# Token attention in a four-layer gated block: mask on four diagonal pieces, division after the weighted sum, head-wise exponentials, and the routing of two chunks inside the second attention

## What is computed

```python
x = x + tanh(g_xattn[1]) * L1_xattn(layernorm(x), ctx, ...)   # "attention(1)"
x = x + tanh(g_ffn[1])   * L1_ffn(layernorm(x), ...)          # experts, top 2 of 8
x = x + tanh(g_xattn[2]) * L2_xattn(layernorm(x), ctx)        # token attention
x = x + tanh(g_ffn[2])   * L2_ffn(layernorm(x), ...)          # "ffn2"

def L2_xattn(q, k, v):       # per token: its 16 heads attend to one another
    scores = einsum('bsqd,bskd->bsqk', qh, kh) / sqrt(8)       # 16 x 16 per token
    scores = where(tril(ones((16, 16))), scores, -1e18)
    return einsum('bsqk,bskd->bsqd', softmax(scores), vh)
```

## Time and profile before

| | |
|---|---|
| median of 3 runs | 1651.29 us (1651.13 to 1655.38) |
| the profiled execution | 1648.97 us, its span 1647.2 us |
| PE busy | 1186.6 us, 72% of the span |
| DVE busy | 1185.9 us, 72% |
| POOL busy | 790.9 us, 48% |
| ACT busy | 699.4 us, 42% |

### The profile page before, as it was taken

One profiled execution on the slowest core, in us unless ns is written; L12 is line 12 of the kernel. 1 busy time (PEld: TensorE's weight loads), 2 busy tenths in 40 slices (PEclk: granted clock), 3 DMA queues, 4 the chain that ended last, 5 costly groups with the idle time before them and its releaser, 6 DMA issues. The chain is left out here.

```text
span 1647.2 us, 31338 instructions
## 1 busy us (share of the span) xinstructions
PE 1186.6 (72%) x9741; PEld 789.5 (48%) x9741; DVE 1185.9 (72%) x3134; ACT 699.4 (42%) x1333; POOL 790.9 (48%) x834
## 2 busy tenths in 40 slices
PE   3788885459989869988886342404899886887886
PEld 1455554136656547756654111101566664544554
DVE  5677876686757635368888787885767565998997
ACT  1455554126656434455555111101566553333332
POOL 0223320003343137677777867873234323776876
PEclk9999998569999889989999665556999998999998
DMA  8455553253545023312112000310444420000000
GB/s 195 60 87 69 72 111 118 33 156 56 81 55 69 17 77 99 95 39 58 46 46 64 24 3 13 50 53 0 66 72 71 58 40 1 1 14 1 13 14 13
DMA packets 95266, 90.99 MB, mean 55 GB/s; under 512 B 8928, under 2 KB 85344, under 8 KB 94816
## 3 DMA queue, kind: packets, MB, share of 16 engines
q1 hardware_dynamic: 91040, 80.98, 26.2%
q0 software_dynamic: 4096, 8.40, 1.7%
HBM read 32.72 MB, written 18.87 MB: 31 GB/s over the span
## 5 line engine op out<-in xcount | busy, mean ns | idle before, releaser
L1533 DVE TENSOR_REDUCE neg_max<-bank 128x4 f32<-128x512 f32 x384 | 252.5, 686 | 129.2 <-PE bank L1053 127.1
L824 ACT ACTIVATE probs<-bank 128x512 f32<-128x512 f32 x384 | 212.5, 596 | 167.3 <-PE bank L1080 166.3
L1051 PE MATMUL bank<-mask_b,ident_b 128*128 128x512 bf16 x384 | 153.4, 400 | 67.0 <-DMA k_rows<-area 37.0
L555 POOL TENSOR_SCALAR rstd_a<-meanvar 128x4 f32<-128x4 f32 x48 | 12.0, 250 | 299.6 <-DVE meanvar L1489 221.0
L1053 PE MATMUL bank<-k_rows,q_rows 96*128 96x256 bf16 x768 | 153.9, 283 | 0.0
L817 ACT ACTIVATE q_rows<-bank 32x512 bf16<-32x512 bf16 x192 | 103.0, 582 | 107.3 <-PE bank L1063 103.9
L606 POOL CAST area<-area 128x1024 bf16<-128x1024 f32 x36 | 37.3, 1036 | 219.8 <-DMA k_rows<-area 167.1
L1070 PE MATMUL bank<-ident_b,mask_b 128*128 128x512 bf16 x384 | 134.3, 391 | 3.0 <-ACT probs L824 1.8
L1080 PE MATMUL bank<-q_rows,k_rows 128*128 128x128 bf16 x1536 | 135.4, 222 | 0.0
L1080 PEld LDWEIGHTS bank<-q_rows,k_rows 128*128 128x128 bf16 x1536 | 112.1, 99 | 27.7 <-issue 2.8
L1094 PE MATMUL bank<-probs,v_aug 128*32 128x128 f32 x3072 | 112.2, 287 | 0.8
(11 more groups left out here) (253 smaller groups left out, 3013.4 us busy)
## 6 DMA issues: line engine op xcount, KB each, us to landing
q_rows<-area SPq DMA_DIRECT2D x144, 128.0 KB
k_rows<-area SPq DMA_DIRECT2D x288, 64.0 KB
ctxT<-ctx_t SPq DMA_DIRECT2D x24, 256.0 KB, 6.7
moe_rows<-m2b SPq DMA_DIRECT2D x4, 1536.0 KB, 13.5
q_rows<-moe_rows SPq DMA_DIRECT2D x24, 256.0 KB, 3.2
moe_rows<-work SPq DMA_DIRECT2D x24, 256.0 KB, 2.4
room<-w_exp SPq DMA_DIRECT2D x1, 4352.0 KB, 13.6
mask_i<-mask SPq DMA_DIRECT2D x8, 256.0 KB, 8.5
```

Source lines behind the costliest of these rows:

```text
L824: act.activation(probs[j].rearrange("p a b -> p (a b)"), T_BANK[j % 2][:], ACT.Exp).then_inc(exp_done, 1)
L1051: pe.matmul(dst[:], ident_b[:], bcast(mask(b, t), 4), start=True, stop=False)
L1533: dve.tensor_reduce(neg_max[:, 4 * j:4 * j + 4], S_BANK[j % 2][:].rearrange("p (h k) -> p h k", h=4), AX.X, ALU.max, negate=True).then_inc ...
```

## The change

**Routing.** Chunk 0 is now routed wholly in the group `left` = 1 of `attention(1)` and chunk 1 in the group `left` = 0, up to its choice; chunk 1's ranks open PE's expert stage and its `put` opens DVE's. The scatter of chunk 0 stands on POOL at the head of the group `left` = 0, ahead of the bias additions. In the blocks only chunks 2 and 3 are left: statistics in blocks 0 and 1, turns and logits in blocks 1 and 3, choice and places in blocks 2 and 4. Chunk 1's scatter is split in two, with the inverse deviation of chunk 3 between the halves. Chunk 3's rows move to the room of the token products, so `products(0)` waits for its scatter. `FIRST_STEP` is 8: tiles 0 to 15 run in blocks, 16 to 31 in the tail, and the first four groups of ffn2 come one tile later in the tables.

**Token attention.** The mask is added to the 4 × 4 pieces on the diagonal only (64 scores; the rest of `tok_raw` is filled with the masked value once). `probabilities` is gone. The weighted product takes the exponentials themselves, in two buffers that alternate, and waits for `token_exp`; in `combine` DVE makes the sum and the reciprocal ahead of its wait for the weighted product, and a new product of 128 × 128 with the reciprocal stands behind the reductions. For n ≥ 16 there is no subtraction: ACT makes 16 exponentials, one per head, with the negated maximum as bias. The factor 1/√8 moves into the norm ahead of the products.

**POOL's order.** A half of the next group's gather stands between products(n+1) and weighted(n), not behind weighted(n).

```diff
-FIRST_STEP = 9
+FIRST_STEP = 8
+TAIL = NK - FIRST_STEP
+        tok_weights = (tok_e, tok_p)
...
 # POOL, attention(1)
+                        if a == 1 and left == 0:
+                            scatter(0)
                         if not is_first:
                             for t in range(TG):
                                 add_bias(TG * (gr - 1) + t)
-                        if a == 1 and left == 0:
+                        if a == 1 and left == 1:
                             route_std(1)
-                            scatter(0)
...
 # POOL, weighted(n)
-                pool.wait_ge(tok_probs, n + 1)
+                pool.wait_ge(tok_exp, n + 1)
...
 # POOL, feed_forward1_and_tokens
-                scatter(1)
+                scatter(1, range(TG))
                 route_std(3)
+                scatter(1, range(TG, TC))
...
+                    if g + 1 < NG and t < 2:
+                        gather(g + 1, range(2 * t, 2 * t + 2))
                     for events in (FFN2_STATS, NEXT_STATS):
                         if n in events:
                             at += 1
                             inv_std(at)
                     weighted(n)
-                    if g + 1 < NG:
-                        if t < 2:
-                            gather(g + 1, range(2 * t, 2 * t + 2))
...
 # ACT, token_exp(n)
-                act.activation(tok_e, tok_s, ACT.Exp, scale=DH ** -0.5).then_inc(tok_exp, 1)
+                weights = tok_weights[n % 2]
+                if n < TAIL:
+                    act.activation(weights, tok_s, ACT.Exp).then_inc(tok_exp, 1)
+                    return
+                for h in range(H):
+                    ins = act.activation(weights[:, h, 0:h + 1], tok_raw[:, h, 0:h + 1], ACT.Exp, bias=tok_m[:, h:h + 1])
+                ins.then_inc(tok_exp, 1)
...
 # DVE, blocks
+                put(1)
                 for k in range(NK):
...
-                        probabilities(n)
...
 # DVE, score(n), combine(n)
+                if n:
+                    dve.wait_ge(tok_exp, n)
...
+                step(dve.tensor_tensor(own, own, on_diagonal(rows[:, a:a + 4 * (4 * H + 4)]), ALU.add))
+                if n >= TAIL:
+                    dve.tensor_reduce(tok_m, tok_raw, AX.X, ALU.max, negate=True).then_inc(tok_shifted, 1)
+                    return
...
+                step(dve.tensor_reduce(tok_d, tok_weights[n % 2], AX.X, ALU.add))
+                step(dve.reciprocal(tok_d, tok_d))
                 dve.wait_ge(ctx_tok_read, n + 1)
...
+                step(dve.tensor_tensor(tok_o, tok_o, along(tok_d, DH), ALU.mult))
```

More of the change, by code:

```diff
@@ L557, in inv_std, with inv_std_of @@
                 pool.tensor_tensor(rstd[:], rstd_a[:], minus_half[:, 0:TG], ALU.pow).then_inc(rstd_ready, 1)
-            def inv_std_of(variance, part, result, ready, done, count):
+            def inv_std_of(variance, part, result, ready, done, count, scale=1.0):
                 pool.wait_ge(ready, count)
                 waits_apart(pool)
-                pool.tensor_scalar(part, variance, LN_EPS, None, ALU.add).then_inc(pool_steps, ch.one())
+                pool.tensor_scalar(part, variance, LN_EPS, scale, ALU.add, ALU.mult).then_inc(pool_steps, ch.one())
                 pool.wait_ge(pool_steps, ch.count)
@@ L570, in token_std, with scatter @@
             def token_std(g):
-                inv_std_of(t_meanvar[:, :, 1], t_rstd_a, t_rstd, t_stats_ready, t_rstd_ready, g + 1)
-            def scatter(c):
+                inv_std_of(t_meanvar[:, :, 1], t_rstd_a, t_rstd, t_stats_ready, t_rstd_ready, g + 1, float(DH))
+            def scatter(c, tiles=range(TC)):
                 pool.wait_ge(placed, c + 1)
@@ L577, in scatter @@
                 waits_apart(pool)
-                for o in range(2 * TC):
+                for o in (2 * t + k for t in tiles for k in range(2)):
                     t = o // 2
@@ L758, in feed_forward1_and_tokens @@
                 token_std(0)
+                pool.wait_ge(scattered[3], 16 * 2 * TC)
                 products(0)
@@ L848, in body @@
                             has_prev = not (is_first and t == 0)
-                            if a == 1 and left == 0 and t == 1:
-                                gap_weight(0)
+                            if a == 1 and left < 2 and t == 3:
+                                gap_weight(1 if left == 0 else 0)
                             take_max(n, b, t, 0)
@@ L858, in body @@
                             exp(n, 1)
+                            if a == 1 and left < 2 and t == 1:
+                                take_routed(2 - 2 * left)
                             if has_prev and a > 0:
@@ L866, in body @@
                                 take_k(gr + 2)
-                            if a == 1 and left == 1 and t in (1, 2):
-                                take_routed(t - 1)
+                            if a == 1 and left < 2 and t == 1:
+                                take_routed(3 - 2 * left)
                 walk(act, body)
@@ L1165, in body @@
                                 turn_heads(n - 1)
+                            if a == 1 and left < 2 and t == 1:
+                                if left == 1:
+                                    pe.wait_ge(prep_read, 8 * NG)
+                                    pe.wait_ge(experts_loaded, 32)
+                                turn_routed(0 if left == 1 else 2)
+                            if a == 1 and left < 2 and t == 2:
+                                logits(0 if left == 1 else 1)
+                            if a == 1 and left == 1 and t == 3:
+                                ranks(0)
                             scores_t(n, b, t, 0)
@@ L1349, in feed_forward1 @@
                             turn_blk(k + 1)
-                        if m == 2 and k in (0, 2, 4):
-                            logits(k // 2 + 1)
                         if i >= 2:
@@ L1356, in feed_forward1 @@
                     if k in (1, 3):
-                        turn_routed(k + 3)
+                        logits(k // 2 + 2)
                 turn_hidden(NB - 2)
@@ L2021, in score, with combine @@
                 dve.wait_ge(tok_scored, n + 1)
[L2022 to L2039 removed]
+                own = on_diagonal(probs_room[:, 1280:1280 + 4 * (4 * H + 4)])
+                a = ROWS["heads_causal"][0]
+                step(dve.tensor_tensor(own, own, on_diagonal(rows[:, a:a + 4 * (4 * H + 4)]), ALU.add))
+                if n >= TAIL:
+                    dve.tensor_reduce(tok_m, tok_raw, AX.X, ALU.max, negate=True).then_inc(tok_shifted, 1)
+                    return
+                step(dve.tensor_reduce(tok_m, tok_raw, AX.X, ALU.max))
+                dve.tensor_tensor(tok_s, tok_raw, along(tok_m, H), ALU.subtract).then_inc(tok_shifted, 1)
+            def combine(n):
+                dve.wait_ge(tok_exp, n + 1)
+                step(dve.tensor_reduce(tok_d, tok_weights[n % 2], AX.X, ALU.add))
+                step(dve.reciprocal(tok_d, tok_d))
                 dve.wait_ge(ctx_tok_read, n + 1)
```

115 lines of the change are left out of this document (44 added, 71 removed).

## The result

The changed kernel takes 1632.75 us (median of 4 runs, 1629.07 to 1635.71) against 1653.22 for the kernel before, measured beside it: a ratio of 0.9879, 95% interval 0.9852 to 0.9905. That is 20.5 us less where 32.7 were forecast, inside the stated range and above its middle.

A forecast was written before the change was run, and what follows sets the result against it. No engine is full; the passing of work between engines sets the pace, judged by four chains. −8.6 − 10.5 − 1.6 − 12 = −32.7, so 1618.6 us against the median of 1651.29; range 1598 to 1638.

The forecast's parts named there:

- A: Into the expert stage: chunk 0's earlier routing and scatter bring block 0's first product near 591; −8.6 us (−10 to −4).
- B: First product to first token add: two chunks fewer to route in the blocks; −10.5 us (−15 to −6).
- C: Sixteen token tiles at block pace: four tiles in 50 us instead of 51.35; −1.6 us in all (−8 to +4).
- D: Sixteen token tiles in the tail: no probabilities step, no subtraction, gather moved; −12 us (−20 to −4).
- the probabilities step now leaves the way to the weighted product: Tiles in blocks: sum, reciprocal and product, some 1.1 us a tile, no longer precede POOL's weighted product; 4.3 for four tiles.
- half of the mask's own time: Tiles in blocks: half of the mask's 0.944 us is port waiting that stays, so the 64-element mask was priced at 0.45.
- The wait on block 11's rows in block 12: POOL stands once before the third group's gather, as block 11's rows are stored only in block 12; +2 us (0 to 5).
- The last cut: Tiles 28 to 31 in the tail: from 37.63 to 29.7 us, nearly POOL alone.
- the first and third cut: In the tail, tiles 16 to 18 from 48.39 to 46.5 us, and tiles 22 to 24 from 49.04 to 48.6.
- rival 1: Routing pays, tokens don't: gather and multiply eat the shorter chain's gain, C and D at zero; 1632 us, chance 0.17.
- Rival 4: Slower: new multiply and following add each wait for a POOL product, about 2.5 us on 32 tiles; 1663 us, chance 0.06.

The follow-up runs named there:

- tokens-alone kernel: The new token attention and gather order put into the kernel before, with its old routing and first token tile in block 9: 1640.12 us, ratio 0.9927.
- routing alone: The changed kernel with token functions and the gather's place taken from the kernel before, ffn2 tables as changed: 1635.08 us, ratio 0.9878.
- kernel with the gather behind: The changed kernel with the halves of the gather put back behind weighted(n) on POOL, all else kept: 1643.45 us, ratio 0.9932.

## Why the prediction was right in A and B and wrong in C and D

- **A, −8.6, measured −7.4.** The scatter starts at 553.14 (forecast 555), the last DMA is issued at 572.43 (574), the first product stands at 592.34 (591). PE's wait is gone; the placing of chunk 1 is what came last, as named. The mechanism is right: from the attention's last addition to the first product 9.8 us went (15.55 to 5.73), and all the other traces with the new routing have 5.7 to 5.9. The size of the whole term is less sure. In this pair the attention grew by 2.4 (its last addition at 586.61, before at 584.17) where 1.5 was charged; but the tokens-alone kernel, with the old routing, has that addition at 578.20, and the traces with the new routing have it from 584.79 to 592.32. So the agreement to 1.2 us is partly luck, and whether the attention grew by over 5, which was named as a sign of being wrong, these traces leave open. The time of the routing alone (1635.08 against 1653.39) bears out A and B together.
- **B, −10.5, measured −11.1.** 88.0 us from the first product to the first add, forecast 88.6. Right in its parts too: chunk 3 is placed at 647.4, 55.1 after the first product (forecast 55), and the add follows 33.0 later (33.6).
- **C, −1.6 (−8 to +4), measured +7.1.** The step that failed is "the probabilities step now leaves the way to the weighted product, 4.3 for four tiles". It left the way, but four tiles still take 51.40 (end of tile 5's weighted product at 772.38, of tile 9's at 823.78; 51.35 before). These two tiles don't show the loss itself, as the moved gather shifts them within their group: from the first add to the end of tile 3's weighted product, and on to those of tiles 7, 11 and 15, it is 64.7, 54.3, 52.5 and 52.8 us, before 63.4, 51.3, 51.5 and 50.8. The weighted product that comes sooner, or is pushed by the gather, joins POOL's next products, and a step of DVE stands still for both. I had the port in the text and priced it as half of the mask's own time, 0.25 on each tile, from a row of the tail; in the tail the mask did come to 0.43, in the blocks it stayed at 0.94. The rows here have single steps of 2.5 to 4.7, which stand beside a run of POOL and not beside one instruction. Adding the wait back shows the size: with the gather behind, 15.4 us between the kernels that differ by it. The wait on block 11's rows in block 12 was forecast at 2 and is 3.08 (the profile names no releaser for it; SP issues that block's store at 748.49):

```profile
745.05 3.50 POOL L739 TENSOR_TENSOR probs<-xnT,v_aug 128x128 f32<-128x128 f32 x4
751.62 1.07 POOL L601 DMA_INDIRECT ctxT<-moe_rows,m2b  x1 [3.08 <-issue]
```

- **D, −12, measured −8.3.** The mechanism was partly another one. I gave most of the gain to the probabilities and booked the moved gather as a cost, 5 us of issue ahead of a weighted product, and only one wait of 4.53 as its gain; the runs say that the gather's place is the gain (7.2 to 10.5) and the arithmetic gives nothing or some 2. The DMA waits of before (4.53 at 949.69, and two more of 4.54 and 3.38) are what went: the additions of gathered rows wait 0.1 for DMA in the tail now. The last cut was forecast at 29.7, with 2 more for tile 31, and took 39.92; that is more than the whole miss of 3.7, and the first and third cut, 3.4 and 2.6 shorter than forecast, hide a part of it. Tile 30, ACT and POOL:

```profile
1098.90 0.69 ACT L976 ACTIVATE hq<-bank,cols 128x512 fp8e4<-128x512 f32 x1 [0.57 <-PE bank L1395]
1099.48 3.16 ACT L917 ACTIVATE probs<-probs,mask_i 128x1 f32<-128x1 f32 x16
...
1102.72 3.83 POOL L753 TENSOR_TENSOR prod<-probs,q_rows 128x128 f32<-128x128 f32 x4 [7.45 <-ACT probs L917]
```

  The sixteen exponentials take 3.16 (forecast 3.0), but they stand on ACT behind ffn2's activations of group 6, which wait for PE; POOL waits 7.45. The prediction looked at DVE and POOL in these tiles and not at ACT's order. It named the sign, POOL waiting for the exponentials, as what would prove it wrong.
- **The rivals.** The time is that of rival 1, 1632 (routing pays, tokens don't), and C and D together are −1.2 where it had zero; but the two don't stand still, one loses 7.1 and the other gains 8.3. Rival 4's mechanism (multiply and addition standing behind POOL) was found in the kernel with the gather behind, up to 6.66 us a step. In the changed kernel itself the multiply takes 0.43 to 0.46 on average, inside the forecast 0.3 to 0.9, and the addition 1.2 in eight tiles of the tail.
- **The rule of the Trainium skill** ("SBUF — State Buffer", "Who interferes with whom") that was weighed holds in its direction: in the blocks the mask's wait did stay when the mask shrank (1.02 to 0.94), though not in the tail (0.94 to 0.43). That reductions never contend agrees with the 0.22 of all 32. That the loser waits for the other's whole instruction is too little here: 7.20 and 7.37 us span eight instructions of POOL.

What stays open: the exact length of C does not follow from the sum of the long waits alone. With the reduction in place of the mask they make 23.5 us at C = 218.9, in the changed kernel 23.1 at 224.2. How much of a wait reaches the block's pace depends on what is queued behind it in that block, and that was not taken apart.

## What to carry to other kernels

Taking a wait out of the way of an engine can cost more than it gives, when that engine then works through, back to back, just while another has steps that stand still beside it: look at what the freed engine will run beside, and not only at what it had waited for. When a step of DVE is shrunk to a quarter and takes as long as before, it is standing, and a still smaller step won't help: here another kind of step (a reduction) or another order on POOL did. A transfer wants to be issued early where the engine that issues it would wait anyway (the tail) and late where it sets the pace (the blocks): the same move was worth −7 to −10 us in the one stretch and between nothing and +12 in the other.

## What the runs showed of the hardware

- A DVE addition, subtraction or multiply that meets POOL's two-operand products can stand beside up to eight of them in a row: 0.42 of work took 4.69, 0.35 took 6.63, 0.42 took 7.37.
- An addition of a constant, which reads a single tile of 64 scores, waits in the same way, 7.20 us; a reduction over the same scores takes 0.22 each time.
- Activations of 1 to 16 columns with a bias from a tile take 0.287 each on average (L917), and sixteen in a row 3.16.
